# Reordering the expert blocks of the first mixture, with the first batch's attention preparation beside the last nine

## The reference

```python
# x: [4, 1024, 128]; layernorm without parameters is ln()
x = x + 0.5 * ffn(ln(x))      # mixture of 8 experts, the best 2 of 8 per token
x = x + attention(ln(x))      # 16 heads of 8, q = k = v = ln(x) @ W_qkv.T
x = x + 0.5 * ffn(ln(x))      # the same weights again
def ffn(x):
    xf = ln(x) * g + b
    scores, idx = top_k(xf @ router_w, 2); gate = softmax(scores)
    # each expert: (clip-silu gated) 128 -> 512 -> 128 on ln(xf)
    return sum over experts of gate[e] * expert_e(xf)
```

## Time and profile before

| what | us |
|---|---|
| median of 3 runs | 1428.36 (1426.97 to 1428.97) |
| the profiled execution | 1427.73 |
| its span | 1426.0 |
| PE busy | 1248.9 (88%) |
| DVE busy | 1170.2 (82%) |
| ACT busy | 896.2 (63%) |
| POOL busy | 511.2 (36%) |
| first block's first chunk on PE starts | 109.50 |
| last gate of the first mixture (ACT L1299) starts | 330.98 |
| first row maximum on PE starts | 371.11 |
| first score on PE starts | 398.87 |
| second mixture's first chunk starts | 1167.25 |

### The profile page before, as it was taken

The page is one execution under the profiler, slowest core; times in us unless marked ns, Lnnn a source line. Parts: engine busy times, 40 slices in busy tenths (PEclk is TensorE's granted clock), DMA queues, the critical chain, the costliest instruction groups (busy, mean ns, idle before and its releaser), DMA issues.

```text
span 1426.0 us, 29423 instructions
## 1 busy us (share of the span) xinstructions
PE 1248.9 (88%) x10053; PEld 649.7 (46%) x10053; DVE 1170.2 (82%) x2305; ACT 896.2 (63%) x1876; POOL 511.2 (36%) x595
## 2 busy tenths in 40 slices
PE   3738999984389999999999999999999988889992
PEld 3727888872022222322323323233322247778882
DVE  8876788876698899889898988988899458868885
ACT  1214555552058888888778887788877865545651
POOL 3875333334433000243335324351434023433331
PEclk9999999996589999999999999999999999999997
DMA  8126545451311201102111011011101312445555
GB/s 260 38 71 217 203 180 191 178 204 34 104 51 35 72 19 35 36 24 66 36 40 48 17 57 36 17 52 36 36 3 32 113 62 101 161 170 186 188 204 192
DMA packets 65382, 135.58 MB, mean 95 GB/s; under 512 B 13330, under 2 KB 34932, under 8 KB 65204
## 3 DMA queue, kind: packets, MB, share of 16 engines
q1 hardware_dynamic: 56196, 116.18, 23.7%
q0 software_dynamic: 8704, 16.93, 3.7%
q10 hardware_dynamic: 336, 0.59, 0.1%
HBM read 47.35 MB, written 25.07 MB: 51 GB/s over the span
## 4 chain that ended last, share of the span: by engine, by line
PE 44%; DVE 21%; DMA 3%; issue 3%; ACT 3%; SPq 1%; POOL 0%; ACTq 0%; POOLq 0%; DVEq 0%
PE psum L2067 13%; DVE att_neg_part L1753 11%; PE psum L2043 7%; PE psum L2047 5%; PE psum L2024 5%; PE psum L1971 3%; PE psum L1959 3%; PE psum L1961 3%; DVE att_neg_part L1758 2%; DVE stats L1426 1%; ACT att_probs L1326 1%; DMA y_dram<-ffn_y,ffn_block_rows 1%; PE psum L2090 1%; ACT att_o_t L1341 1%; DMA ffn_rec<-record 1%
## 5 line engine op out<-in xcount | busy, mean ns | idle before, releaser
L1326 ACT ACTIVATE att_probs<-psum 128x512 f32<-128x512 f32 x1024 | 556.5, 596 | 119.3 <-PE psum L2049 90.3
L1753 DVE TENSOR_REDUCE att_neg_part<-psum 128x2 f32<-128x1024 f32 x441 | 532.0, 1223 | 69.0 <-PE psum L2025 56.0
L2067 PE MATMUL psum<-att_probs,att_values 128*16 128x256 f32 x4096 | 321.4, 386 | 6.3 <-ACT att_o_t L1341 4.2
L1281 ACT ACTIVATE ffn_silu<-ffn_x2c,ffn_rec 128x256 f32<-128x256 f32 (+1 forms) x320 | 154.6, 487 | 163.3 <-DVE ffn_x2c L1689 162.6
L1143 POOL DMA_INDIRECT y_dram<-ffn_y,ffn_block_rows x144 | 142.1, 987 | 274.5 <-ACT ffn_y L1299 248.7
L2024 PE MATMUL psum<-att_right,att_left 64*128 64x512 bf16 x512 | 198.3, 388 | 27.5 <-DMA att_right<-q_parts_dram 15.9
L2043 PE MATMUL psum<-att_right,att_left 64*128 64x512 bf16 x512 | 198.6, 388 | 4.9 <-DVE att_neg_part L1753 4.8
L2046 PE MATMUL psum<-att_right,att_left 64*128 64x512 bf16 x512 | 198.5, 388 | 4.0 <-DVE att_neg_part L1753 2.1
L1689 DVE TENSOR_SCALAR ffn_x2c<-psum,ffn_rec 128x256 f32<-128x256 f32 (+1 forms) x320 | 162.8, 513 | 45.9 <-PE psum L1961 41.7
L2025 PE MATMUL psum<-att_right,att_left 64*128 64x512 bf16 x512 | 198.9, 389 | 0.0
L2047 PE MATMUL psum<-att_right,att_left 64*128 64x512 bf16 x512 | 193.7, 378 | 0.0
(11 more groups left out here) (198 smaller groups left out, 1514.4 us busy)
## 6 DMA issues: line engine op xcount, KB each, us to landing
ffn_rec<-record SPq DMA_DIRECT2D x80, 776.5 KB, 3.7
ffn_block_rows<-rows_dram SPq DMA_DIRECT2D x64, 130.0 KB, 2.2
att_left<-q_parts_dram SPq DMA_DIRECT2D x64, 96.0 KB
att_right<-q_parts_dram SPq DMA_DIRECT2D x120, 48.0 KB
record<-in_L_ffn_W SPq DMA_DIRECT2D x16, 256.0 KB, 6.5
last_y<-y_dram SPq DMA_DIRECT2D x8, 512.0 KB, 7.4
att_right<-q_parts_dram SPq DMA_DIRECT2D x90, 32.0 KB
y_dram<-ffn_y,ffn_block_rows POOLq DMA_INDIRECT x144, 2.6
```

The lines of the kernel that those rows point to most:

```text
L1326: S.activation(probs[:, slot % PROBS, :], ring_bank(("score", slot))[:, :], ACT.Exp, scale=SCALE).then_inc(att_bank.by_act, 1)
L1753: last = V.tensor_reduce(out=neg_part[:, h % 2, keys, p::PAIR, t], in_=psum[:, low:high + 1, :], axis=AX.X, op=ALU.max, negate=True)
L2067: last = TE.matmul(value_bank[head * VS:head * VS + VW, q], values[:, b % 2, kt, team * TEAM + head, :], probs[:, (UNIT * n + j) % PROBS, ...
```

## The change

The 40 blocks come in another order in both mixtures: 23 pairs, then the 8 single blocks, then 9 pairs (`SINGLES` = blocks 23 to 30). In each expert the pairs that hold rows of the first batch are given out first, so that all results of batch 0 are there after block 30. For that, `vector_pairs` and `vector_places_of_blocks` work on 16 columns (8 experts, twice) in place of 8. Of the first mixture's transition, the following moves into its blocks, by a new list `HEAD` with one entry per chunk from block 23 on: POOL's blanking of `values` 0 and 1 and of the left and right operand of set 0 (at blocks 23, 24, 25, 26); the whole preparing of batch 0, from block 34, chunk 3, to block 38, chunk 0; SP's loads of batch 0's results, after block 34's loads; the writing of q's parts and the loading of the left operand and six right pieces, after block 39's loads. The attention weights are loaded, transposed and copied at the start of the program. Rows and records get slots of their own: 6 for rows, 4 (first mixture) or 6 (second) for records; a record is loaded once the block that many before it has its bias applied (`biased`), and the order is record first, then rows. The preparing uses PSUM bank 7 alone (`side_bank`). POOL's blanking of sets 1 and 2 stays where it was.

```diff
+    LEFT = E - 2
+    SINGLES = slice(EARLY + LEFT, EARLY + LEFT + E)
+    SECTIONS = [slice(0, EARLY), slice(EARLY, SINGLES.start), SINGLES, slice(SINGLES.stop, BLOCKS)]
+    SLOTS = (4, 6)
+    ROW_SLOTS = 6
...
+        HEAD = [[] for _ in range(HC * (BLOCKS - SINGLES.start))]
+        for n in range(4):
+            HEAD[4 * n].append(("blank", n, 0, WHOLE))
+        at = HC * E
+        for step, half, slot in ((0, 0, 15), (1, 0, 15), (0, 1, 16), (1, 1, 16), (2, 0, 17), (2, 1, 18), (11, 0, 23), (11, 1, 25)):
+            HEAD[at + slot].append(("prepare", 0, step, (half, 2)))
+        for step, slot in ((3, 19), (5, 20), (7, 21), (9, 22), (13, 27), (15, 28)):
+            HEAD[at + slot].append(("prepare", 0, step, WHOLE))
...
             for i in range(EARLY, BLOCKS):
                 sync_next_block(k, i)
+                if k == 0 and i == SINGLES.stop + SLOTS[0] - 1:
+                    sync_first_results()
+            if k == 0:
+                sync_first_team()
...
         def sync_next_block(k, i):
-            n = k * BLOCKS + i - SLOTS
-
-            Q.wait_ge(scattered_y[n % YSETS], y_scatters(n + 1, n % YSETS))
+
+
+            Q.wait_ge(biased, k * BLOCKS + i - SLOTS[k] + 1)
+            sync_load_record(k, i)
+            if i >= ROW_SLOTS:
+                n = k * BLOCKS + i - ROW_SLOTS
+                Q.wait_ge(scattered_y[n % YSETS], y_scatters(n + 1, n % YSETS))
             sync_load_rows(k, i)
-            sync_load_record(k, i)
+
+        def sync_first_results():
+
+            for r in range(YSETS):
+                Q.wait_ge(scattered_y[r], y_scatters(SINGLES.stop, r))
...
+        def sync_first_team():
+
+            sync_ones(0)
+            sync_write_parts(0, 0)
+            sync_operand_lefts(0)
+            for n in FIRST_RIGHTS:
+                Q.dma_start(*right_load(0, n)).then_inc(first_pair_in, 16)
+            sync_write_parts(0, 1)
...
             for r in range(YSETS):
                 G.wait_ge(scattered_y[r], y_scatters(BLOCKS, r))
-            pool_blank_values(0)
-            pool_blank_left(0)
-            for chore in PREPARED:
-                pool_chore(*chore)
-            pool_blank_right(0)
-            G.wait_ge(split_done, 1)
-            pool_blank_values(1)
             for s in range(1, OPERANDS):
                 pool_blank_left(s)
                 pool_blank_right(s)
...
         def tensor_turn(k, i):
             n = k * BLOCKS + i
-            TE.wait_ge(block_in[seat(i)], 32 * block_loads(n))
+            TE.wait_ge(mix[k].rows_in[i % ROW_SLOTS], 16 * (i // ROW_SLOTS + 1))
...
         def vector_attention():
-
-            V.wait_ge(product, BLOCKS)
-            V.wait_ge(weighed, BLOCKS)
-            for r in range(YSETS):
-                V.wait_ge(scattered_y[r], y_scatters(BLOCKS, r))
-            V.memset(value_bank[:, :], 0.0).then_inc(value_bank_blanked, 1)
-            for chore in PREPARED:
-                vector_chore(*chore)
+            V.wait_ge(*when_emptied(("prepare", 0, 15)))
             for n in range(MAX_FIRST):
                 vector_row_max(n)
+                if n == 0:
+                    V.memset(value_bank[:, :], 0.0).then_inc(value_bank_blanked, 1)
```

More of the change, by code:

```diff
@@ L244, in build_macaron @@
         first = ExitStack()
-        sets.extend(RouteSet(k, first) for k in range(1, B - 1))
-        beyond = sbuf("beyond_the_blocks", [P, 4096], owner=first)
-        sets.append(RouteSet(B - 1, first))
+        last_set = RouteSet(B - 1, first)
         VEC = 2 * E + 2 * E * HC + E
@@ L1073, in pool_chore @@
                 G.tensor_tensor(rows, rows, projected(half), ALU.add).then_inc(x_by_pool, 1)
+            elif what == "blank" and which < 2:
+                pool_blank_values(which)
+            elif what == "blank" and which == 2:
+                for lane in sets[B - 1].rows_out:
+                    G.wait_ge(lane, 16 * BT)
+                pool_blank_left(0)
+            elif what == "blank":
+                pool_blank_right(0)
             elif what == "mix":
@@ L1614, in vector_pairs @@
-            settle(V.tensor_scalar(ends[:, n, 1:E + 1], ends[:, n, 1:E + 1], float(most), None, ALU.min))
+            settle(V.tensor_tensor(both[:, 0:E], firsts_f[:, :], pairs_f[:, :], ALU.min))
+            settle(V.tensor_tensor(both[:, E:2 * E], pairs_f[:, :], both[:, 0:E], ALU.subtract))
+            settle(V.tensor_tensor_scan(ends[:, n, 1:2 * E + 1], twice[:, :], both[:, :], 0.0, ALU.mult, ALU.add))
+            settle(V.tensor_scalar(ends[:, n, 1:2 * E + 1], ends[:, n, 1:2 * E + 1], float(most), None, ALU.min))
```

309 lines of the change are left out of this document (162 added, 147 removed).

## The result

| | before | changed |
|---|---|---|
| median of 7 runs, us | 1426.97 (1423.1 to 1428.97) | 1434.83 (1431.88 to 1435.07) |
| ratio | | 1.0053, 95% interval 1.004 to 1.0067 |
| span of the profiled execution | 1426.0 | 1433.3 |

The change makes the kernel 0.5% slower. The forecast was 1415.5 and 0.8% faster, the range 1404 to 1423: wrong in size and in sign.

The account below looks back on a forecast made before the run. PE bounds the kernel except in the hole before the attention. First score -17.0, lay-outs +2.3 and +2.5, second mixture -2.0, -1.5 and +3.3 sum to -12.4 us: 1415.5 us forecast, range 1404 to 1423.

Parts of the forecast that it names:

- The hole: First mixture to attention: row maxima start at about W, the last gate's end, not W + 39.8 us.
- What is late next: Behind W, POOL's memsets then SP's issues delay the first score to W + 39.5, 11 us of new idle time.
- rival A: SP's queue isn't late, or chores cost only their least: score at W + 28.5, 1404.5 us; chance 0.12.
- term (a): First mixture's fillers, issued earlier with four record slots: PE's stand shrinks to 1.2 us, -1.5 (-2.7 to +2).
- Term (b): First mixture's single blocks: records about -4 us, POOL's memsets holding clips +4, sum 0 (-3 to +7).
- rival C: First mixture's rows land late behind records: at 5.6 us the gain is gone and 3 us more, 1431; chance 0.04.
- rival B: POOL's work beside blocks holds DVE for its full length, 10.8 us in place of 4: +8, 1423.5; chance 0.18.
- Term (c): Batch 0's preparing from block 34 on: 13.2 us more DVE work, PE's 3.5 us lying under it, costs +10.5.
- Term (d): First mixture's last block is now a pair, with a longer second product and steps around it: +2 us.
- Lay-outs and the end: Early lay-out in the attention +2.3, late one in the second mixture +2.5, its last block a pair +3.3 us.
- The second mixture's fillers: PE's stand of 4.03 us behind the fillers shrinks, as its turn waits for rows alone: -2 (-3 to 0).
- Its singles' records: Second mixture's records of singles are issued a block sooner: -1.5 of 2.2 us.

Follow-up runs that it names:

- SP's order: Changed kernel with SP issuing set 1's loads and the first place before set 2's ones and batch 1's results: 1423.6 us, 0.9976 of the kernel before (first chip).
- all five mends: Changed kernel plus SP's order, fine pieces, spread preparing, batch 0's adds on POOL, rows ahead of records: 1406.79 us, 0.9852 of the kernel before (first chip).
- fine pieces: Changed kernel with POOL's blanking of values and set 0 in 50 pieces from block 6 on: 1427.21 us, 1.0001 of the kernel before (first chip).
- double_dve: Changed kernel with statistics, `xh`, first cast and first subtraction of batch 0 done twice on DVE: ratio 1.0054 to the kernel before (third chip).

## Why the prediction was wrong

**The hole: right.** Row maxima started 0.06 us after the last gate ended, and all of batch 0's parts and operands were there.

**What is late next: right, a little under.** POOL began at W + 5.4 (forecast 4.25), its eight memsets took 14.8, SP's issues ran on to W + 35.0 (33.85), and place and return took 7.4 us (forecast 5.6): the write's issue lasted 2.25 us in place of 0.31. Score at W + 42.5, forecast 39.5. The run with SP's order shows that the wait is removable and worth 11.2 us (1434.83 to 1423.6), as rival A's price said.

**W, term (a), fillers: wrong sign.** Forecast -1.5, measured +1.3 between blocks 0 and 21. With four record slots the fillers' 9.5 us start 11.5 us earlier, but two blocks sooner PE needs the loads that stand behind them; it stood 2.41 us for rows, and block 2 came 4.0 us late where before block 4 came 2.9 late. Here too rows stand behind records: in the version with all five mends, rows first among them, the stretch takes 119.8, 1.2 us less than before, near the 1.5 forecast.

**Term (b), singles: the step that failed most.** I wrote +4 for the memsets ("if each catches a clip half-way") and -4 for the records, sum 0; measured +9.9, of which 1 belongs to the pairs. The records' -4 is the larger miss. PE's 4.3 us of stands for records did go, but stands for rows took their place, since the rows now stand behind the records and their wait: 3.2 us in the singles and 1.5 right after, and 5.4 once the memsets no longer covered them. With fine pieces the stretch is 3.3 us above before, not 4 below, or 2.3 without the pair's 1 us; with rows first as well it is 37.2 against 37.6, so at most 1.4 of the 4 us come. That was rival C on a small scale.

It isn't the landing that I had wrong: rows behind records landed in 3.0 to 3.2 us at the median, 1.8 to 2.2 before, and C took 3 to 4. It is the lead: I had argued it from pairs ("some 7 us before PE turns block i"), and single blocks come at half that distance.

The memsets cost 6.6 us on the first chip (7.6 by the medians, 1434.83 to 1427.21) where I had 4: clips were held 9.5 us, not 5.4. Four memsets caught a clip of y nearly whole, 2.49 us for a clip of 0.29, two a clip of the hidden values half-way; in other traces of the same memsets it was 5.3 us, my own guess, so the mean was a fair centre and a poor bound. That was rival B's mechanism; I had row and price (1.90 us).

The Trainium skill (SBUF — State Buffer, section "SBUF: two separate sides") says that GpSimd and a two-port VectorE instruction hold the shared ports for a whole instruction; the traces agree: the clips from SBUF to SBUF end 0.1 to 0.3 us behind their memset, the combines from PSUM keep their length.

**Term (c), chores: the cover failed.** Forecast +10.5, measured +16.7, of which 1.7 is the step with the stand for rows; the 1 us from the singles comes on top. I took 0.83 us per us of DVE's work from the second mixture's tail, where the chores are spread over 33 chunks, and let PE's own 3.5 us of products "lie under this, as DVE is the bound there". They did not. 5.66 us of DVE's work stand in two chunks; PE used up its lead, stood 4.73 us, and then had the block's matmuls, the turning of `xh` and the projection before it, the first 5.57 us at half its clock, with DVE waiting for PE in turn. That step costs 6.05 us, 3.2 by PE's products and 2.8 by the clock, which the sum had at nothing. My own "without that cover they come on top, 14.5" was nearer. Added DVE work cost 1.14 us per us (double_dve), and 4.5 us were won for 2.8 taken off, both with a share of the clock that one trace each doesn't separate. Spreading gave back 4 us in its stretch.

**Term (d), the drain: right by luck in part**, +2.5 for +2. The granted clock was 0.58 over these last 5.3 us, and the last product took 3.01 us; in three other traces it took 1.99, and block 39 to W 4.0 us, only 1.2 more than before.

**Lay-outs and the end: right** (+1.9, +2.4, +3.0 for +2.3, +2.5, +3.3). **The second mixture's fillers** gave more than said (-4.3 for -2): PE stood 1.41 us in place of 4.03, and the product behind the stand took 1.89 in place of 2.83. **Its singles' records** gave nothing (+0.1 for -1.5): PE stood 3.0 us there for rows in place of 2.4 for records, since the rows still wait for the scatter of the block six before.

The sum: forecast -12.4, measured +7.3. The miss of 19.7 is singles 9.9, pairs 6.2, queue 3.0, fillers 2.8, less some 2 of small terms. Rivals B (0.18) and, weakly, C were both true at once; I had priced them singly, as if only one could be, and closed the range at 1423. On top of the forecast, B's +8 and 5 us of C's stands give 1428.5, and the slower outcome had 0.05. A sign that hangs on several costs of 5 to 10 us each, none of which the trace of before can show, deserved a wider range.

## What to carry to other kernels

Work that is moved from an idle hole to beside a tuned loop isn't hidden by the average slack of its engine: ask for each piece at which moment it comes, which instruction stands behind it on its own engine and on the one that shares its ports, and cut it small enough for the smallest slack. After taking a hole away, read every queue again from the new point: here 11 of the 40 us went straight into SP's, by an order that had cost nothing before. When a long instruction of one engine and a short one of another stand at the same place of a loop, they meet, and how much of the long one is waited for changes with the run (5.3 to 9.5 of 11.0 us here): put the whole into the range. And a wait that is taken away shows the next one behind it: ask what PE would wait for if the records came at once.

## What the runs showed of the hardware

- A DVE clip of 0.29 us beside a POOL memset took 2.49; cut in eight, the memsets held it hardly at all (300 ns on average), though they came back to back with gaps of 0.06 us. But a 64x256 memset costs 0.30 us where an eighth of the long one is 0.23, and a 128x256 one 0.36 where an eighth is 0.23, so the cut costs POOL a third to a half more time.
- After PE had had no work for 4.70 us, eight matmuls took 3.78 us in place of 1.89, and the granted clock was 0.50 for 5.57 us. A stand of 7.73 us was followed by one of 3.66, one of 1.90 by 3.40, but another of 1.89 by 2.00, and a stand of 2.49 by 1.99 in one trace and 3.46 in another: how short a stand costs the clock isn't settled by these runs.
- The same kernel before took 1427 us on the first chip and 1490 to 1497 on two others, with the clock cut inside the attention. The ratios agree within their intervals: 1.0053 (1.004 to 1.0067) and 1.0032 (1.0011 to 1.0053) for the changed kernel, 0.9852 and 0.9826 for the best version.
